# A graph layer's edge tables: edges sorted upwards, and the first blocks' tables, gathers, statistics and one-hots made beside the table stage

## Chip, cores and metric

One core of a Trainium2 chip. The metric is the device time of one execution in microseconds (us); lower is better.

## What is computed

The input is `x` (50000 nodes x 128), 25000 edges with a node `src` each and an attribute row `edge_attr` (25000 x 128), and the weights of a small network.

```
h   = relu(layernorm(x))
agg = segment_sum(edge_attr, src, 50000)          # edge rows added up per node
z   = silu(concat(h, agg) @ W1 + b1) @ W2 + b2    # 256 -> 256 -> 128
out = x + h + layernorm(z) * gamma + beta
```

`dst` is not used in the result. `src` is uniformly random over the nodes and not sorted.

## The kernel before

**Tiles and blocks.** Nodes are worked on in 49 blocks of 1024 (`BLOCK`), a block is 8 tiles, a half is 4 tiles. A tile is 128 nodes, or 128 slots for edge rows. There are NT = 392 tiles.

**Table stage (to 88 us).** Which edge rows belong to which tile must first be found out. The 25000 edges lie as 125 rows of EC = 200 columns. VectorE sorts each row by node: a key holds the node and the column, `largest` (MAX8) takes eight keys, `strike` (MATCH_REPLACE8) removes them. The sorted columns come in 50 groups of 4 (`STREAMS`). Since a sorted row of random nodes runs evenly through all nodes, column n needs only a window of the tiles (`WINDOWS`, at most 160 of 392); the largest nodes come first, so the windows go downwards. One `group_step(g)` on VectorE (L1001) makes the tile one-hots of group g (`hot_tile`, L1018), does its share of the sort and, for group g - 3 (`LAG_SLOT`), copies the ranks (L978), compares them with slot numbers (`is_slot`, L987) and multiplies with the edges' words (`hot_slot`, L996). TensorE does three matmuls for a column: `before` (L667) counts the edges of a tile in the rows above, `others` (L660, 4 columns later) adds the rest, the third (L673, 16 columns later) adds the word to a table in PSUM. ScalarE reads one rank per column out of the counts (L521). A loop of 200 + 16 columns on TensorE and of 200 on ScalarE, with waits on semaphores, keep the three in step. VectorE may run ahead until it meets the copy of ranks of group g - 3.

**Hand-over (88 to 110 us).** When the last column is through, ScalarE copies the last counts (L527), VectorE adds them up (`total_of`, L1040) and both copy the tables to SBUF (L1045, L537); ScalarE adds up how many edges found no slot (`excess_of`) and prepares the second layer's weights and the halves of the first's (`w1h`, means, `w2c`, `b2c`: L541 to L548). TensorE puts the words in their rows (L687), and VectorE makes from them the edge number of each slot: `table_words` and `edge_fields` for the first three blocks (24 tiles), then the first four tiles' edge numbers (`first_edge`, L1108), on which GpSimd starts four gathers (`gather_first`, L462). VectorE goes on with the statistics of block 0 (`statistics`, L871), `powers` (reciprocal square roots in 11 linked small steps and some more, L902 to L929; each linked step waits for the one before), `spill_flags`, `slot_tables`, the one-hots of block 0 (`one_hots`, L1122), and the low half of W1 (`w1l`, L1171). If an edge found no slot (it doesn't happen with these inputs), GpSimd adds up all edges one by one in HBM instead (`add_up_spill`). TensorE runs 24, 4 and 4 dummy matmuls (`keep_busy`, L693) ahead of and between its first pieces.

**Block stage.** For each half of a block TensorE turns h (`turn_h`, L702) and sums the gathered rows by one-hots (`sum_edges`, L717) into `za`; ScalarE rounds `za` to `hi` (L564, L566), VectorE makes the rest `lo` (`split_low`, L1132); TensorE's first layer takes `hi` and `lo` (`pre`, L731 to L736), ScalarE applies silu (L573), TensorE's second layer gives `y` (L756), ScalarE sums its squares (L603), and VectorE scales, adds h, x and beta (L1144, L1161, L1139, L1114). GpSimd gathers each tile's edge rows with one indirect DMA (L454). SyncE loads and stores blocks.

**What sets the order.** Each engine's program is a list written out by hand. An engine does its own list in order; a wait holds up all that stands behind it. The order of VectorE's list around the change is: all of `group_step`, totals and words, tables, L1164 to L1176, then `step(b)` from L1178, which for block 0 makes the word tables of the other 46 blocks, for block 1 their edge numbers.

Of the kernel before, what the change touches and what calls it, by code (L numbers as in the profile page):

```python
# [38 lines left out]
COLUMN_BITS = 8  # L39

# [59 lines left out]
def gnn_layer(nc, x, src, edge_attr, W1, b1, W2, b2, gamma, beta, out):  # L100
# [36 lines left out]
    assert SORTS[-1].stop == EC and WINDOWS[0].stop == NT  # L137
# [3 lines left out]
    with ExitStack() as ctx:  # L141
# [61 lines left out]
        first_part = sb("first_part", [P, HALF], F32)  # L203
        first_edge = sb("first_edge", [P, HALF], U32)
# [56 lines left out]
        dve_step, sort_step = sem("dve_step"), sem("sort_step")  # L261
        unpacked, fields_made, words_ready = sem("unpacked"), sem("fields_made"), sem("words_ready")
        w1h_ready, w1l_ready, means_ready, w2c_ready = sem("w1h_ready"), sem("w1l_ready"), sem("means_ready"), sem("w2c_ready")
# [109 lines left out]
        def _(pool):  # L373
            nc.gpsimd.memset(srci[:], OUTSIDE).then_inc(src_filled, 1)
            small_iota = dict(allow_small_or_imprecise_dtypes=True)
            nc.gpsimd.iota(column_no[:], [[1, EC]], base=1, channel_multiplier=0)
# [11 lines left out]
            for tiles_here in (WINDOWS[0], slice(0, WINDOWS[0].start)):  # L388
# [16 lines left out]
            def add_up_spill():  # L405

                pool.wait_ge(late_const, 1)
                rows_zeroed = P * TILES
# [37 lines left out]
            def gather(b, c, source, limit, pacer=None, signal=None):  # L446

                if b.is_number(FIRST_BLOCKS) and c == 0:
                    pool.wait_ge(slots_ready, 2)
# [9 lines left out]
            def gather_first(limit):  # L459

                for t in range(HALF):
                    nc.gpsimd.indirect_dma_start(  # L462
                        G[0][:, t, :], None, edge_attr,
                        bass.IndirectOffsetOnAxis(ap=first_edge[:, bass.ds(t, 1)], axis=0),
                        bounds_check=limit, oob_is_err=False).then_inc(first_gathered[t], 16)

            def gather_rest(source, limit):

                pool.wait_ge(slots_ready, 1)
                gather(Block(0), 1, source, limit)  # L470
                for c in range(2):
                    gather(Block(1), c, source, limit)

                def step(b):
                    if b.plus(2).exists(NB):
# [20 lines left out]
            with pool.If(flag != 0):  # L496
                spill_limit = pool.to_reg(NB * BLOCK - 1)
                add_up_spill()
                for t in range(HALF):
                    pool.wait_ge(first_gathered[t], 16)  # L500
                pool.wait_ge(slots_ready, 1)
                gather(Block(0), 0, spill, spill_limit, signal=gathered_anew)
                pool.wait_ge(gathered_anew, 16 * HALF)
# [5 lines left out]
        def _(act):  # L509
# [15 lines left out]
            run_columns(rank_of, 0)  # L525
# [8 lines left out]

            excess_of(0)
            act.wait_ge(slot_free, EC + UNROLL)
            nc.scalar.copy(words[:, 1, :], table[1][:, 0:NT]).then_inc(words_copied[1], 1)  # L537
            excess_of(1)

            act.wait_ge(weights_loaded, 16 * 6)  # L540
            nc.scalar.copy(w1h[:], w1f[:]).then_inc(w1h_ready, 1)  # L541
            for m in range(2):
                nc.scalar.activation(junk_w[:, m, :], w2f[:, m, :], ACT.Copy, scale=-1.0 / D, accum_out=w2mean[:, m:m + 1])
            nc.scalar.activation(junk_w[:, 2, :], b2f[:], ACT.Copy, scale=-1.0 / D, accum_out=b2mean[:]).then_inc(means_ready, 1)
            act.wait_ge(means_ready, 1)
            for m in range(2):
                nc.scalar.activation(w2c[:, m, :], w2f[:, m, :], ACT.Identity, bias=w2mean[:, m:m + 1])
            nc.scalar.activation(b2c[:], b2f[:], ACT.Identity, bias=b2mean[:]).then_inc(w2c_ready, 1)  # L548
# [39 lines left out]
            def bias(b, c):  # L588

                if b.is_number(0) and c == 0:  # L590
                    act.wait_ge(w2c_ready, 1)
# [713 lines left out]
```

## Time and profile before

| | us |
|---|---|
| median of three runs | 709.94 |
| lowest and highest | 709.68, 710.02 |
| the profiled execution | 710.16 |
| span of the profile in it | 708.6 |
| TensorE busy | 679.5 (96%) |
| VectorE busy | 688.1 (97%) |
| ScalarE busy | 608.5 (86%) |
| GpSimd busy | 479.6 (68%) |
| mean granted TensorE clock | 0.97 |

The profile covers one execution. The span runs from the first to the last instruction; the execution's own time is 1.56 us longer. PE is TensorE, PEld its weight loads, DVE is VectorE, ACT ScalarE, POOL GpSimd, SP SyncE. A busy time is the time in which records of an engine's instructions lie; records of neighbouring instructions may overlap by some 0.1 us. The granted clock is 1.00 for 2.4 GHz and 0.50 for 1.2 GHz. Times in a timeline row are its start and its length in us.

### The profile page before, as it was taken

The page shows a single profiled execution, that of the slowest core. Times are in us where ns is not written, and L with a number is a line of the kernel's source. Part 1 is how long each engine was busy: PE and PEld are TensorE (multiplying, and loading weights), DVE is VectorE, ACT ScalarE, POOL GpSimd, SP SyncE. Part 2 cuts the span into 40 slices and gives each one's busy share as a digit, 9 for nine tenths or more (in the row PEclk, how much of TensorE's full clock was granted, in tenths as well). Part 3 has the DMA queues.
Part 4 walks back from the last instruction along what each step waited for, and adds up shares of the span by engine and source line. Part 5 has one row for each costly group of instructions (what it writes and reads, how often), then busy time and mean ns, then how long its engine had stood idle before and what let it go on. Part 6 is the DMA issues. An engine that isn't in the chain of part 4 may idle for free.

```text
span 708.6 us, 15614 instructions
## 1 busy us (share of the span) xinstructions
PE 679.5 (96%) x4566; PEld 597.0 (84%) x4566; DVE 688.1 (97%) x2361; ACT 608.5 (86%) x2090; POOL 479.6 (68%) x416
## 2 busy tenths in 40 slices
PE   5999988799999999999999999999999999999993
PEld 3888847698998989898989898999998989899983
DVE  8999879999999999999999999999999999999998
ACT  7999957598898989898989898989898989889883
POOL 5000057687777787777778787778787778777850
PEclk7799979899999999999999999999999999999997
DMA  6000001133333333332424242424232423331212
GB/s 221 1 1 2 1 16 53 52 123 101 118 108 112 111 106 122 95 130 83 140 84 141 83 141 83 140 83 141 84 138 85 132 92 123 104 106 53 81 42 84
DMA packets 28260, 65.90 MB, mean 93 GB/s; under 512 B 8469, under 2 KB 10023, under 8 KB 28174
## 3 DMA queue, kind: packets, MB, share of 16 engines
q1 hardware_dynamic: 15598, 51.90, 20.7%
q0 software_dynamic: 12576, 12.99, 7.6%
q8 instruction: 37, 0.61, 0.4%
q14 instruction: 49, 0.40, 0.2%
HBM read 52.05 MB, written 25.60 MB: 110 GB/s over the span
## 4 chain that ended last, share of the span: by engine, by line
DVE 67%; issue 20%; PE 11%; ACT 1%; DMA 0%; DVEq 0%; POOL 0%; POOLq 0%
DVE T L1144 14%; DVE lo L1132 10%; DVE stat L871 10%; DVE R L1114 8%; DVE R L1139 8%; PE y L673 3%; DVE R L1161 2%; PE za L660 2%; PE pre L667 2%; PE pre L660 2%; PE za L667 1%; DVE guess_off L924 1%; PE pre L693 1%; DVE mdd L907 1%; DVE var L910 1%
## 5 line engine op out<-in xcount | busy, mean ns | idle before, releaser
L454 POOL DMA_INDIRECT G<-in_edge_attr_dram,slot_edge x388 | 465.7, 1200 | 121.0 <-issue 90.2
L756 PEld LDWEIGHTS y<-w2c,S 128*128 128x128 f32 (+1 forms) x1556 | 188.2, 191 | 8.0
L756 PE MATMUL y<-w2c,S 128*128 128x128 f32 (+1 forms) x1556 | 189.2, 275 | 0.0
L556 ACT ACTIVATE H<-X,shift,rstd 128x128 f32<-128x128 f32 x392 | 161.9, 489 | 4.4 <-DVE shift L929 4.4
L731 PE MATMUL pre<-hi,w1h 128*128 128x512 f32 (+1 forms) x392 | 163.8, 418 | 0.0
L732 PE MATMUL pre<-hi,w1l 128*128 128x512 f32 (+1 forms) x392 | 154.6, 394 | 0.0
L573 ACT ACTIVATE S<-pre,b1c 128x512 f32<-128x512 f32 (+1 forms) x196 | 125.4, 700 | 4.5 <-PE pre L736 4.5
L736 PE MATMUL pre<-lo,w1h 128*128 128x512 f32 (+1 forms) x392 | 123.1, 395 | 0.1
L1132 DVE TENSOR_TENSOR lo<-za,hi 128x1024 fp32r<-128x1024 f32 (+1 forms) x98 | 119.1, 1216 | 2.4 <-ACT hi L566 2.4
L871 DVE BATCH_NORM_STATS2 stat<-X 128x6 f32<-128x128 f32 x392 | 106.8, 281 | 0.1
L717 PE MATMUL za<-HOT,G 128*128 128x128 f32 (+1 forms) x784 | 104.7, 277 | 0.9 <-DMA G<-in_edge_attr_dram,slot_edge 0.9
L1144 DVE SCALAR_TENSOR_TENSOR T<-y,rstd,gammas 128x128 f32<-128x128 f32 x384 | 103.5, 342 | 0.0
L595 ACT COPY y<-b2c 128x512 f32<-128x512 f32 x97 | 59.1, 609 | 49.8 <-DVE T L1144 49.8
L603 ACT ACTIVATE junk_sq<-y 128x128 bf16<-128x128 f32 x388 | 99.7, 268 | 1.5 <-PE y L756 1.5
L717 PEld LDWEIGHTS za<-HOT,G 128*128 128x128 f32 x784 | 96.2, 193 | 1.7 <-DMA G<-in_edge_attr_dram,slot_edge 1.5
L736 PEld LDWEIGHTS pre<-lo,w1h 128*128 128x128 f32 x392 | 73.7, 188 | 18.7 <-DVE lo L1132 1.0
L731 PEld LDWEIGHTS pre<-hi,w1h 128*128 128x128 f32 x392 | 74.4, 190 | 13.5 <-ACT hi L566 0.3
L732 PEld LDWEIGHTS pre<-hi,w1l 128*128 128x128 f32 x392 | 74.3, 190 | 13.3
L603 ACT ACTIVATION_READ_ACCUMULATOR junk_sq<-y 128x1 f32 x388 | 78.8, 203 | 0.0
L566 ACT CAST hi<-za 128x512 fp32r<-128x512 f32 (+1 forms) x98 | 57.5, 587 | 16.2 <-PE za L717 16.2
L702 PE MATMUL za<-ident,H 128*128 128x128 f32 (+1 forms) x392 | 60.4, 277 | 6.7 <-DVE lo L1132 6.7
L564 ACT CAST hi<-za 128x512 fp32r<-128x512 f32 (+1 forms) x98 | 58.9, 602 | 6.2 <-PE za L702 6.2
(160 smaller groups left out, 953.2 us busy)
## 6 DMA issues: line engine op xcount, KB each, us to landing
X<-in_x_dram SPq DMA_DIRECT2D x48, 512.0 KB, 3.6
out_dram<-R SPq DMA_DIRECT2D x48, 512.0 KB
G<-in_edge_attr_dram,slot_edge POOLq DMA_INDIRECT x388, 2.6
X<-in_x_dram SPq DMA_DIRECT2D x1, 424.0 KB
out_dram<-R SPq DMA_DIRECT2D x2, 192.0 KB
w1f<-in_L_gnn_W_dram SPq DMA_DIRECT2D x1, 256.0 KB, 2.7
w2f<-in_L_gnn_W_dram SPq DMA_DIRECT2D x1, 128.0 KB, 2.7
srci<-in_src_dram SPq DMA_DIRECT2D x1, 87.5 KB
```

Source lines behind the costliest of these rows:

```text
L454: nc.gpsimd.indirect_dma_start(G[b.j][:, t, :], None, source, bass.IndirectOffsetOnAxis(ap=slot_edge[:, bass.ds(b.number(TILES, t), 1)], a ...
L556: done = nc.scalar.activation(H0[b.j][:, t, :], X[b.xj][:, t, :], ACT.Relu, bias=shift[b.j][:, t:t + 1], scale=rstd[b.ring(POWERS_LAG)][:, ...
L573: nc.scalar.activation(S[c][:, m, w], pre[m][:, w], ACT.Silu, bias=b1c[:, m:m + 1]).then_inc(silu_done, 1)
L603: done = nc.scalar.activation(junk_sq[:, p, c * HALF + t, :], y[2 * p + c][:, t * D:(t + 1) * D], ACT.Square, scale=float(D) ** -0.5, accu ...
L717: done = nc.tensor.matmul(za[:, 1, t * r:(t + 1) * r], G[b.j][:, c * HALF + t, :], HOT[b.j][:, c * HALF + t, 0:r], start=True, stop=True)
L731: nc.tensor.matmul(pre[m][:, w], w1h[:, k, cols], hi[c][:, k, w], start=(k == 0), stop=False)
L732: nc.tensor.matmul(pre[m][:, w], w1l[:, k, cols], hi[c][:, k, w], start=False, stop=False)
L736: done = nc.tensor.matmul(pre[m][:, w], w1h[:, k, cols], lo[c][:, k, w], start=False, stop=(k == 1))
L756: done = nc.tensor.matmul(places[t][0:r], S[c][:, m, t * r:(t + 1) * r], w2c[:, m, :], start=False, stop=True, skip_group_check=True)
L871: done = nc.vector.bn_stats(stats[b.ring(2)][:, t, :], X[b.xj][:, t, :])
L1132: nc.vector.tensor_tensor(out=lo[c][:, :, w], in0=za[:, :, w], in1=hi[c][:, :, w].bitcast(F32), op=ALU.subtract).then_inc(lo_done, 1)
L1144: done = nc.vector.scalar_tensor_tensor(out=T[c][:, t, :], in0=y[2 * b.ring(2) + c][:, t * D:(t + 1) * D], scalar=rstd[b.ring(POWERS_LAG)] ...
```

## The change

The edges are sorted upwards: the key is negated and brought above zero by a constant, and taken back when it is made an integer. The windows now start at tile 0 and end at tile 392. With that, the first three blocks' tiles (`FIRST` = 24) get no more edges after group READY - 1 (READY = 12, so EARLY_AT = 16, statistics from group 22, powers from group 30). At group 16 VectorE copies these 24 columns of the tables; TensorE places the words at column 64; VectorE makes the edge numbers in the steps of groups 17 to 21, the statistics of block 0 after groups 22 to 29, its powers around groups 30 to 40, its one-hots after that. GpSimd gathers all 24 tiles from `first_edge`. ScalarE prepares the weights beside columns 16 to 40. After the last column VectorE copies the other 368 columns and fixes the slots of blocks 1 and 2; 3 dummies stand where 24 stood, and the last 4 are gone.

```diff
-                first = max(0.0, 1.0 - middle - reach) * nodes
-                final = min(1.0, 1.0 - middle + reach) * (nodes - 1)
+                first = max(0.0, middle - reach) * nodes
+                final = min(1.0, middle + reach) * (nodes - 1)
+    FIRST = FIRST_BLOCKS * TILES
+    READY = max(g for g in range(GROUPS) if WINDOWS[g].start < FIRST) + 1
+    EARLY_AT = READY + LAG_SLOT + 1
+    EARLY_STEPS = 6
+    STATS_AT = EARLY_AT + EARLY_STEPS
+    POWERS_AT = STATS_AT + TILES
...
 # GpSimd
             def gather_first(limit):
-                for t in range(HALF):
+                for n in range(FIRST):
+                    b, t = Block(n // TILES), n % TILES
+                    done = first_gathered[t] if n < HALF else gathered[b.j][t // HALF]
                     nc.gpsimd.indirect_dma_start(
+                        G[b.j][:, t, :], None, edge_attr,
+                        bass.IndirectOffsetOnAxis(ap=first_edge[:, bass.ds(n, 1)], axis=0),
+                        bounds_check=limit, oob_is_err=False).then_inc(done, 16)
             def gather_rest(source, limit):
-                pool.wait_ge(slots_ready, 1)
-                gather(Block(0), 1, source, limit)
-                for c in range(2):
-                    gather(Block(1), c, source, limit)
...
 # ScalarE
-            run_columns(rank_of, 0)
+            def weights_beside(column):
+                for m in range(2):
+                    if column.is_number(16 + 4 * m):
+                        nc.scalar.activation(junk_w[:, m, :], w2f[:, m, :], ACT.Copy, scale=-1.0 / D, accum_out=w2mean[:, m:m + 1])
+                    if column.is_number(32 + 4 * m):
+                        nc.scalar.activation(w2c[:, m, :], w2f[:, m, :], ACT.Identity, bias=w2mean[:, m:m + 1])
+                if column.is_number(24):
...
+                if column.is_number(28):
+                    act.wait_ge(means_ready, 1)
...
+                if column.is_number(40):
+                    nc.scalar.copy(w1h[:], w1f[:]).then_inc(w1h_ready, 1)
...
+            normalise(Block(0), 0)
+            for s in range(PAIRS):
+                excess_of(s)
+            normalise(Block(0), 1)
             split_high(Block(0), 0)
...
 # TensorE
+            def place_words(at, copied):
+                for i in range(PAIRS):
+                    pe.wait_ge(words_copied[i], copied)
...
+                        done = nc.tensor.matmul(slot_word[w][:, at], to[rows, :], words[rows, s, at], **add)
...
+                if late.is_number(READY * STREAMS):
+                    pe.wait_ge(late_const, 1)
+                    place_words(slice(0, FIRST), 1)
...
             pe.wait_ge(totals_done, 2)
-            keep_busy(24)
+            keep_busy(3)
             turn_h(Block(0), 0)
             keep_busy(4)
+            pe.wait_ge(words_read, 2)
+            place_words(slice(FIRST, NT), 2)
             sum_edges(Block(0), 0)
-            keep_busy(4)
...
 # VectorE
             def as_integers(at, number):
-                nc.vector.tensor_copy(top_i[:, at], top[:, at]).then_inc(unpacked, 1)
+                nc.vector.tensor_scalar(out=top_i[:, at], in0=top[:, at], scalar1=-1.0, scalar2=float(KEY_TOP),
+                                        op0=ALU.mult, op1=ALU.add).then_inc(unpacked, 1)
...
                 # powers: behind each of its 11 linked steps
+                    if b.is_number(0):
+                        group_step(Item(POWERS_AT + place))
...
+            def copy_words(at, columns_done):
+                dve.wait_ge(slot_free, columns_done)
+                for s in range(PAIRS):
+                    nc.vector.tensor_copy(words[:, s, at], table[s][:, at]).then_inc(words_copied[s], 1)
...
                 # group_step: behind hot_tile
+                    if g.is_number(EARLY_AT):
+                        copy_words(first_tables, UNROLL + READY * STREAMS)
...
+            def early_tables(step):
...
+                if step == 1:
+                    dve.wait_ge(words_placed, 2)
+                    table_words(at)
...
+                elif step == 4:
+                    dve.wait_ge(early_step, 2)
...
+                    or_nowhere(first_edge[:], edge_f[:, at], at).then_inc(first_ready, 1)
...
+            for n in range(EARLY_AT):
+                group_step(Item(n))
+            for n in range(EARLY_STEPS):
+                group_step(Item(EARLY_AT + n))
+                early_tables(n)
             for t in range(TILES):
+                group_step(Item(STATS_AT + t))
                 statistics(Block(0), t)
             powers(Block(0))
-            spill_flags()
-            slot_tables(first_tables)
+            dve.wait_ge(early_step, 4)
+            dve.wait_ge(late_const, 1)
             one_hots(Block(0))
+            for n in range(POWERS_AT + SMALLS, GROUPS + LAG_SLOT):
+                group_step(Item(n))
+            dve.wait_ge(counts_copied, 1)
+            for s in range(PAIRS):
+                total_of(s)
+            copy_words(other_tables, EC + UNROLL)
             dve.wait_ge(w1h_ready, 1)
             nc.vector.tensor_tensor(out=w1l[:], in0=w1f[:], in1=w1h[:].bitcast(F32),
                                     op=ALU.subtract).then_inc(w1l_ready, 1)
+            for t in range(HALF):
+                statistics(Block(1), t)
+            spill_flags()
+            later = slice(TILES, FIRST)
+            link(nc.vector.tensor_scalar(out=slot_node[:, later], in0=slot_node[:, later], scalar1=kept[:],
+                                         scalar2=own_slot[:], op0=ALU.mult, op1=ALU.add))
+            for t in range(HALF, TILES):
+                statistics(Block(1), t)
             split_low(Block(0), 0)
-            for t in range(TILES):
-                statistics(Block(1), t)
             powers(Block(1))
```

Also changed, for the case of an edge without a slot: `add_up_spill` waits for the early gathers and sets tables and one-hots anew, and all three blocks are gathered again.

## Rows read from the trace of the kernel before

**Rows 1.** Windows, one block: us; busy PE, PEld, DVE, ACT, POOL; clock, DMA, GB/s.
```profile
307.73:319.70 11.97, 11.97 (x83) 10.77 (x82) 11.90 (x39) 10.62 (x35) 9.53 (x8) 1.00 0.34 109
```
**Rows 2.** Chain that ended last, hand-over: start us, us, what.
```profile
91.27 7.93 PE pre L693 x24
...
101.42 0.59 ACT hi L566
102.04 1.23 DVE lo L1132
...
108.85 1.23 DVE lo L1132
...
110.85 0.23 PE pre L731
```
**Rows 3.** Waits of VectorE in 8 to 89 us: total us, times, longest.
```profile
DVE rank L978 <- ACT junk_rank L521: 2.2, 8, 0.4
```
**Rows 4.** Timeline of the table stage: groups 16, 17, 41, 49; column 47; last `hot_slot`.
```profile
32.11 0.46 DVE L1018 TENSOR_TENSOR hot_tile<-iota_tile,tile_of 128x608 f16<-128x608 f16 x1
32.41 0.32 PE L673 MATMUL y<-hot_tile,hot_slot 128*128 128x152 f16 x1
33.38 0.49 DVE L1018 TENSOR_TENSOR hot_tile<-iota_tile,tile_of 128x640 f16<-128x640 f16 x1
...
72.83 0.43 DVE L1018 TENSOR_TENSOR hot_tile<-iota_tile,tile_of 128x544 f16<-128x544 f16 x1
...
84.10 0.25 DVE L1018 TENSOR_TENSOR hot_tile<-iota_tile,tile_of 128x192 f16<-128x192 f16 x1
...
88.05 0.42 DVE L996 TENSOR_TENSOR hot_slot<-is_slot,word 128x512 f16<-128x512 f16 x1
```
**Rows 5.** Timeline, VectorE in the hand-over: prices of the moved work.
```profile
94.11 0.17 DVE L903 SCALAR_TENSOR_TENSOR m<-stat 128x8 f32<-128x8 f32 x1
94.19 0.17 DVE L905 TENSOR_TENSOR mdif<-stat 128x8 f32<-128x8 f32 x1
...
103.18 1.63 DVE L871 BATCH_NORM_STATS2 stat<-X 128x6 f32<-128x128 f32 x8
...
105.48 1.22 DVE L1122 TENSOR_TENSOR HOT<-iota_node,slot_node 128x1024 f32<-128x1024 f32 x1
```
**Rows 6.** ScalarE: windows (columns as in rows 1), then timeline, first and last of its weight work.
```profile
14.00:20.00 6.00, 4.77 (x49) 3.92 (x48) 5.90 (x32) 5.50 (x32) 0.00 (x0) 0.50 0.51 200
20.00:25.00 5.00, 4.75 (x40) 4.45 (x41) 4.90 (x26) 4.59 (x26) 0.00 (x0) 0.51 0.01 3
...
90.84 0.60 ACT L541 CAST w1h<-w1f 128x512 fp32r<-128x512 f32 x1
...
92.97 0.39 ACT L548 ACTIVATE b2c<-b2f,b2mean 128x128 f32<-128x128 f32 x1
```
**Rows 7.** Windows of one us; the clock is the third number from the end.
```profile
86.00:87.00 1.00, 1.00 (x12) 0.49 (x10) 0.73 (x4) 1.00 (x10) 0.00 (x0) 0.67 0.00 0
...
96.00:97.00 1.00, 1.00 (x5) 0.36 (x4) 0.86 (x8) 0.26 (x1) 0.86 (x1) 0.71 0.16 32
...
130.00:131.00 1.00, 1.00 (x5) 0.76 (x4) 0.97 (x4) 1.00 (x5) 0.55 (x1) 0.64 0.00 0
```
**Rows 8.** Timeline, eight `za` matmuls at 2.4 GHz and at 1.2 GHz.
```profile
100.33 1.05 PE L717 MATMUL za<-HOT,G 128*128 128x128 f32 x8
...
126.81 1.92 PE L717 MATMUL za<-HOT,G 128*128 128x128 f32 x8
```
**Rows 9.** Waits of TensorE for gathered rows, 100 to 145 us.
```profile
PE za L717 <- DMA G<-in_edge_attr_dram,slot_edge: 0.5, 2, 0.3
```
**Rows 10.** Timeline, gathers on GpSimd beside VectorE in the block stage.
```profile
299.66 2.18 POOL L454 DMA_INDIRECT G<-in_edge_attr_dram,slot_edge  x1 [0.31 <-issue]
299.75 1.22 DVE L1114 TENSOR_TENSOR R<-X,betas 128x1024 f32<-128x1024 f32 x1
...
302.14 1.01 POOL L454 DMA_INDIRECT G<-in_edge_attr_dram,slot_edge  x1 [0.30 <-DVE lo L1132]
```

More of the change, by code:

```diff
@@ L407, in add_up_spill @@
                 pool.wait_ge(late_const, 1)
+                for j in range(RING):
+                    for c in range(2):
+                        if j or c:
+                            pool.wait_ge(gathered[j][c], 16 * HALF)
+                for t in range(HALF):
+                    pool.wait_ge(first_gathered[t], 16)
+                nc.gpsimd.tensor_copy(slot_edge[:, 0:FIRST], own_node[:, 0:FIRST]).then_inc(pool_step, 1)
+                nc.gpsimd.memset(G[RING - 1][:], 0.0).then_inc(pool_step, 1)
+                pool.wait_ge(hot_done, 1)
+                nc.gpsimd.tensor_copy(HOT[0][:], ident[:].unsqueeze(1).to_broadcast([P, TILES, P])).then_inc(pool_step, 1)
+                pool.wait_ge(pool_step, 8)
                 rows_zeroed = P * TILES
@@ L498, in _ @@
                 add_up_spill()
[L499 to L503, printed above, removed]
+                for n in range(FIRST_BLOCKS):
+                    for c in range(2):
+                        gather(Block(n), c, spill, spill_limit, signal=gathered_anew)
+                pool.wait_ge(gathered_anew, 16 * FIRST)
                 pool.sem_inc(way_known)
@@ L653, in _ @@
             pe.wait_ge(dve_const, 2)
+            def place_words(at, copied):
+                for i in range(PAIRS):
+                    pe.wait_ge(words_copied[i], copied)
+                for w in range(2):
+                    rows = slice(w * CAP, (w + 1) * CAP)
+                    for s in range(PAIRS):
+                        to = ident16 if w == s else swap16
+                        done = nc.tensor.matmul(slot_word[w][:, at], to[rows, :], words[rows, s, at], **add)
+                    done.then_inc(words_placed, 1)
             def column_step(column):
@@ L677, in _ @@
             run_columns(column_step, LAG_TABLE)
-            for i in range(PAIRS):
-                pe.wait_ge(words_copied[i], 1)
-            pe.wait_ge(late_const, 1)
-            for w in range(2):
-                rows = slice(w * CAP, (w + 1) * CAP)
-                for s in range(PAIRS):
-                    to = ident16 if w == s else swap16
-                    done = nc.tensor.matmul(slot_word[w][:, 0:NT], to[rows, :], words[rows, s, :], **add)
-                done.then_inc(words_placed, 1)
             def keep_busy(count):
@@ L1033, in _ @@
             tiles(SORTS[0], 0)
-            for n in range(GROUPS + LAG_SLOT):
-                group_step(Item(n))
-            dve.wait_ge(counts_copied, 1)
             def total_of(s):
```

94 lines of the change are left out of this document (49 added, 45 removed).

## The prediction

> **What bounds the kernel now.** I read the stretches first, then the chain of waits, then the engines' timeline around the two places where the chain changes hands.
>
> In the block stage (from about 140 us) a block takes 11.97 us; TensorE is busy for all of it and VectorE for 11.90 [rows 1]. The change touches nothing there, so it can only shift that stage. It must be judged by two spans ahead of it: the table stage, and the hand-over between it and the first blocks.
>
> The table stage ends on VectorE with the last `hot_slot`, at 88.05 + 0.42 = 88.47 us; call this E. The chain then runs through 24 dummy matmuls (7.93 us), block 0's aggregation and its rounding, and reaches `lo` of block 0's first half at 102.04 and of its second half at 108.85 [rows 2, 4]. From E to the first `lo` are 13.57 us, from the first to the second 6.81.
>
> In the table stage VectorE has hardly any slack: it waits for ranks 2.2 us in all [rows 3]. That idle time is the only cover for work put beside the columns. Group 17's `hot_tile` starts at 33.38, group 41's at 72.83, the last group's (49) at 84.10 [rows 4].
>
> **The change, part by part.** The order of the sort mirrors the windows: their widths add up to the same 6632 tiles over the 50 groups (worked out from the window formula). The key's sign and `as_integers` swap one instruction for one. I take 0, with nothing hidden. For that mirror image the first 24 tiles are complete after group 12, whence READY = 12, EARLY_AT = 16, statistics from group 22, powers from 30.
>
> *Added on VectorE in the table stage.* Statistics of block 0: eight in 1.63. One-hots of block 0: 1.14, from the record of 1.22 less the overlap of 0.08 with its neighbour. Small instructions follow each other by 0.08 [rows 5]; powers has 14, and since a group's step now stands between them their mutual waits go: 14 x 0.085 = 1.2. Early tables are 11 instructions, three of which read PSUM: 0.97. Sum 4.95. Two copies of 24 table columns at group 16: 0.25.
>
> *A new wait at group 16.* `copy_words` waits until the table matmul of column 47 is through. That one starts at 32.41 and takes 0.32; VectorE would be at that point 0.4 after `hot_tile` 16 at 32.11, so at 32.5 [rows 4]. It waits 0.3 even if nothing else moves. Everything of VectorE is queued behind it, `hot_tile` 17 first, for which TensorE then waits. TensorE in turn waits for the copies before four small matmuls; it has no lead to lose there that VectorE doesn't lose too, so I count no second time.
>
> *ScalarE's weight work beside columns 16 to 40.* It takes from 90.84 to 93.36 now, less a short wait, 2.3 us [rows 6]. In 14 to 25 us ScalarE is idle for 0.50 + 0.41 = 0.9 [rows 6], and TensorE needs a rank only four columns later. So between 0 (all hidden) and 1.4 (2.3 - 0.9) is passed on to TensorE and from it into VectorE's wait at group 16. I take 0.5, as the four columns between take up some half microsecond of the rest.
>
> *What goes.* With 4.95 more work VectorE runs behind ranks that are long there, and the 2.2 us of waits vanish. Between groups 17 and 41 it needs 1.64 us a group ((72.83 - 33.38) / 24, some waits included [rows 4]); with 1.0 more over five groups, 1.63 over eight and 1.2 over eleven it needs some 1.75 to 1.85. TensorE and ScalarE would have to need more than that for VectorE to meet a rank wait again, and then they would have held it up more than 2.2 us already.
>
> So E moves by 0.3 + 0.5 + 0.25 + 4.95 - 2.2 = **+3.8**, to 92.3.
>
> *From E to the first `lo`.* Now: totals 1.05 us after E, 24 dummies, `za` of the first half, `hi`. After the change, counted from E: totals done 1.05; three dummies; four transposes; four dummies; four matmuls that place the other words, 0.85; eight `za` matmuls. TensorE's granted clock fell to 1.2 GHz in 86 to 87 us, when the columns got narrow, and rose to 2.4 GHz in 96 to 97, when it had been busy without a gap since 91.2; after the idle time around 124 it rose in 130 to 131, busy since 125.9 [rows 7]. So most of this stretch runs at 1.2 GHz. A dummy costs 0.43 there (5.4 us of them at that pace and the remaining 2.5 at twice the pace make the 24), eight `za` 1.92 against 1.05 [rows 2, 8]. 7 x 0.43 = 3.0, transposes 0.9 (half of eight `za`), words 0.85, `za` some 1.3 with the clock rising inside them, latency 0.15, `hi` 0.6: 1.05 + 3.0 + 0.9 + 0.85 + 1.3 + 0.75 = 7.85, where 13.57 stood: **-5.7**. VectorE is there in time: two totals 0.95, two wide copies 0.9, `w1l` 0.6, eight statistics 1.63, spill flags and the fix of `slot_node` some 0.9, 5.0 after E. The gathers of block 0 are 24 x 1.31 = 31 us from group 20 on, at about 44, so done near 75; `way_known` then hangs on the spill flag alone, some 4.3 after E, under the dummies.
>
> *From the first to the second `lo`.* Eight statistics (1.63) have moved ahead into idle time. But the second half's `hi` isn't earlier by as much: by its own chain (`pre`, transposes, `za`, `hi`) it comes about 5.6 after the first `lo`, with the wait for gathered rows gone [rows 9]. 6.81 to 5.6: **-1.2**. Then TensorE sets `lo` of block 1's first half; there the lead shrinks by **0.5**. Behind that VectorE's own order (tables of the other blocks, statistics, powers) sets the pace as before, and the shift stays.
>
> Sum: 3.8 - 5.7 - 1.2 + 0.5 = **-2.6**. The profiled execution took 710.16 (span 708.6), 0.22 over the median of 709.94. 710.16 - 2.6 = 707.56; the median so 707.3.
>
> **A rule that speaks against the change.** Now 20 more gathers run on GpSimd beside VectorE's dense two-input work. In the trace a gather that starts just ahead of `R` (x plus beta) takes 2.18 instead of 1.01, and `R` its 1.22 as ever; VectorE isn't the one that waits [rows 10]. The Trainium skill, SBUF — State Buffer, "SBUF: two separate sides", says that the port pair shared by GpSimd and VectorE is an exclusive lock: whichever starts first has it for its whole instruction and the other blocks fully. By that rule VectorE would lose up to a gather's length each time; the rows agree for GpSimd as the loser and show no case of the other. My sum goes by the rows.
>
> **The rivals.**
> (a) *The table stage swallows more*: the added instructions fall into latencies between a group's own (a `hot_slot` starts 0.33 after its `is_slot`), and ScalarE passes nothing on. E moves by 1.5 to 2 only. For: VectorE isn't at work in each of those latencies. Against: they stay where they are, since the additions stand behind the group's step. 705.2.
> (b) *The clock or ScalarE's chain takes it back.* 21 of the first dummies and the last four are gone: if the clock rises only behind block 0's first `pre`, its 12 matmuls of 0.23 [rows 2] grow as the eight `za` do (1.92 / 1.05), by 2.3 us, or ScalarE's full 1.4 instead of 0.5 arrives. For: `za` at 126.81 shows what the low clock costs. Against: TensorE has hardly a gap in the stretch. 707.3 + 2.3 = 709.6 for the clock, 708.2 for ScalarE alone.
> (c) *Slower: VectorE blocked by the gathers in the table stage.* 24 gathers of 1.0 us each fall between groups 20 and 45. Each that blocks VectorE for more than 0.11 us on average (2.6 / 24) eats the gain, for more than 0.17 makes it slower by over 0.2%. At half of their length, 12 us: 719; at 0.2 us each: 712. For: the narrow ops there read two SBUF operands most of the time, so a gather will often be first. Against: rows 10, and VectorE's steady rows show the same durations with and without a gather.
> (d) *It doesn't do what it says*: the early gathers come so late that block 0 waits for them. They would need 50 us instead of 31, at more than 2.1 each; then `way_known` is late and the gain shrinks to nothing: 710.
>
> **How the numbers follow.** The forecast has 0.58, (a) 0.14, (b) 0.16, (c) 0.10, (d) 0.02. 0.2% (1.4 us) is about what a measurement of this kernel can tell from no change. Faster takes the forecast and (a) but for 0.02 of the forecast's edge, 0.70; same (b), (d) and that edge, 0.20; slower (c), 0.10. The forecast's own bounds are 706 to 708.9 (0 to 1.4 of ScalarE, 0.5 of pitches, 0.8 of the clock); the range reaches on to (a) and past (b): 704.7 to 710.7.
>
> **What the profile would show.** The last `hot_slot` ends near 92.3, and VectorE has no waits for ranks between groups 17 and 49 (waits there: the step on the table stage is wrong). At group 16 a wait of 0.3 to 1.7 of VectorE on TensorE. Gathers of 1.0 to 1.4 us between 44 and 80. The first `lo` near 100.2 and the second near 105.8; `lo` of block 1 near 111.6 instead of 114.24. The clock back at 2.4 GHz about 6.5 us after E. Blocks still 11.97 us. It is wrong if `hot_tile` or `hot_slot` records lengthen beside gathers, if `za` of block 0 waits for a DMA, or if the block stage's pace changes.

## The result and the profile after

The median after the change is **705.68 us** (four runs, 705.40 to 706.44) against 709.93 for the kernel before in the same comparison: a ratio of 0.9943, 95% interval 0.9931 to 0.9955. That is 4.25 us faster, where 2.6 was forecast. The profiled execution took 705.78, its span is 704.2 (before: 710.16 and 708.6), so the spans differ by 4.4.

The page of the kernel after, busy times:

```profile
PE 675.2 (96%) x4545; PEld 592.5 (84%) x4545; DVE 685.7 (97%) x2360; ACT 607.4 (86%) x2089; POOL 477.8 (68%) x416
```

The busy shares are those of before; nothing there tells where 4.4 us went. The stretches do. One block far inside the block stage, then the steps of one us behind the table stage (columns as in rows 1):

```profile
312.07:324.04 11.97, 11.97 (x82) 10.77 (x81) 11.90 (x39) 10.63 (x35) 9.53 (x9) 1.00 0.33 111
...
14.00:20.00 6.00, 5.20 (x49) 3.67 (x48) 5.89 (x32) 6.00 (x38) 0.00 (x0) 0.50 0.53 212
20.00:25.00 5.00, 4.49 (x37) 3.05 (x38) 4.90 (x26) 5.00 (x28) 0.00 (x0) 0.81 0.01 3
90.00:91.00 1.00, 1.00 (x12) 0.62 (x11) 0.77 (x3) 0.69 (x6) 0.00 (x0) 0.56 0.00 0
...
96.00:97.00 1.00, 1.00 (x5) 0.13 (x4) 0.72 (x4) 0.48 (x2) 0.00 (x0) 0.52 0.00 0
97.00:98.00 1.00, 1.00 (x10) 0.73 (x7) 0.00 (x0) 0.00 (x0) 0.00 (x0) 1.00 0.03 8
```

A block takes 11.97 as in [rows 1]. ScalarE, which had 0.9 us of idle time in 14 to 25 [rows 6], has none left: 6.00 of 6.00 and 5.00 of 5.00. The clock falls at the end of the table stage as it did [rows 7] and is back at 2.4 GHz (1.00) from 97 on, 5.4 us after the table stage's end.

VectorE's timeline of the kernel after: group 16 and the new wait, groups 17, 41 and 49, the last `hot_slot`, the spill flag, and the first, second, third and fifth `lo`. It answers to [rows 4] and [rows 2].

```profile
32.06 0.48 DVE L1058 TENSOR_TENSOR hot_tile<-iota_tile,tile_of 128x640 f16<-128x640 f16 x1
32.97 0.27 DVE L1039 CAST words<-y 128x24 f16<-128x24 f32 x2 [0.42 <-PE y L711]
...
34.04 0.48 DVE L1058 TENSOR_TENSOR hot_tile<-iota_tile,tile_of 128x640 f16<-128x640 f16 x1
...
77.68 0.43 DVE L1058 TENSOR_TENSOR hot_tile<-iota_tile,tile_of 128x544 f16<-128x544 f16 x1
...
87.78 0.25 DVE L1058 TENSOR_TENSOR hot_tile<-iota_tile,tile_of 128x192 f16<-128x192 f16 x1
91.15 0.42 DVE L1028 TENSOR_TENSOR hot_slot<-is_slot,word 128x512 f16<-128x512 f16 x1
95.21 0.15 DVE L1087 CAST spilled_i<-spilled 128x1 int32<-128x1 f32 x1
99.08 1.22 DVE L1155 TENSOR_TENSOR lo<-za,hi 128x1024 fp32r<-128x1024 f32 x1 [2.36 <-ACT hi L587]
104.49 1.22 DVE L1155 TENSOR_TENSOR lo<-za,hi 128x1024 fp32r<-128x1024 f32 x1 [0.58 <-ACT hi L587]
110.41 1.23 DVE L1155 TENSOR_TENSOR lo<-za,hi 128x1024 fp32r<-128x1024 f32 x1 [0.68 <-ACT hi L587]
...
129.01 1.22 DVE L1155 TENSOR_TENSOR lo<-za,hi 128x1024 fp32r<-128x1024 f32 x1
```

VectorE's timeline of the kernel before, the third and the fifth:

```profile
114.24 1.23 DVE L1132 TENSOR_TENSOR lo<-za,hi 128x1024 fp32r<-128x1024 f32 x1
...
133.28 1.22 DVE L1132 TENSOR_TENSOR lo<-za,hi 128x1024 fp32r<-128x1024 f32 x1
```

Call them `lo1`, `lo2`, `lo3` and `lo5`, and E the end of the last `hot_slot`, as in the prediction: 91.15 + 0.42 = 91.57. Then the account is

| stretch | before | after | change | forecast |
|---|---|---|---|---|
| start to E | 88.47 | 91.57 | +3.10 | +3.8 |
| E to lo1 | 13.57 | 7.51 | -6.06 | -5.7 |
| lo1 to lo2 | 6.81 | 5.41 | -1.40 | -1.2 |
| lo2 to lo3 | 5.39 | 5.92 | +0.53 | +0.5 |
| lo3 to lo5 | 19.04 | 18.60 | -0.44 | 0 |
| lo5 to the end of the span | 575.3 | 575.2 | -0.1 | 0 |

Two lines were missed: E moved by 0.7 less than forecast, and 0.44 us came in a stretch that I had declared untouched. The rest of the gap between 2.6 and 4.4 is spread over the hand-over.

The hand-over by TensorE's timeline of the kernel after:

```profile
92.84 1.46 PE L721 MATMUL pre<-zeros 128*128 128x512 f16 x3 [0.85 <-DVE total L1078]
94.10 1.06 PE L730 MATMUL za<-ident,H 128*128 128x128 f32 x4
94.95 1.91 PE L721 MATMUL pre<-zeros 128*128 128x512 f16 x4
96.80 0.39 PE L687 MATMUL y<-words,ident 64*128 64x368 f16 x1
...
97.27 1.16 PE L745 MATMUL za<-HOT,G 128*128 128x128 f32 x8
99.11 0.50 PE L759 MATMUL pre<-hi,w1h 128*128 128x512 f32 x1 [0.68 <-ACT hi L587]
```

From E: 1.27 to the first dummy, 1.26 for three, 0.85 transposes, 1.85 for four dummies, 0.47 words, then 1.16 for `za`, and 0.65 to `lo1`: 7.51.

VectorE's waits of the kernel after, 8 to 95 us and 95 to 152 us; they answer to [rows 3]:

```profile
DVE words L1039 <- PE y L711: 0.4, 1, 0.4
...
DVE lo L1155 <- ACT hi L587: 3.6, 3, 2.4
```

Before, the listed waits for ranks came to 2.2 us [rows 3]; after, one of 0.2 is left, and the wait at group 16 is new.

GpSimd's gathers of the three blocks, first and last of 24, none over 1.19 long:

```profile
42.27 1.16 POOL L482 DMA_INDIRECT G<-in_edge_attr_dram,first_edge  x1 [30.85 <-DVE first_edge L1114]
...
73.80 1.02 POOL L482 DMA_INDIRECT G<-in_edge_attr_dram,first_edge  x1 [0.31 <-issue]
```

### The profile page after: what moved, and what is told of

Same layout as the page of the kernel before. It is cut to its first block, busy times and chain, and to the rows that moved or that the text cites. A ratio compares the mean times of both kernels' runs of the same rounds, so it can differ in the third digit from the quotient of the medians.

```text
span 704.2 us, 15572 instructions
## 1 busy us (share of the span) xinstructions
PE 675.2 (96%) x4545; PEld 592.5 (84%) x4545; DVE 685.7 (97%) x2360; ACT 607.4 (86%) x2089; POOL 477.8 (68%) x416
## 4 chain that ended last, share of the span: by engine, by line
DVE 69%; issue 21%; PE 7%; ACT 2%; DVEq 0%; DMA 0%; POOL 0%; POOLq 0%
DVE T L1167 14%; DVE lo L1155 10%; DVE stat L901 10%; DVE R L1137 8%; DVE R L1162 8%; DVE R L1184 2%; ACT junk_rank L535 2%; PE y L711 1%; DVE guess_off L956 1%; DVE mdd L939 1%; DVE var L942 1%; PE pre L702 1%; DVE hot_slot L1028 1%; DVE keys L857 1%; PE za L695 1%
## 5 line engine op out<-in xcount | busy, mean ns | idle before, releaser
L472 POOL DMA_INDIRECT G<-in_edge_attr_dram,slot_edge x368 | 442.4, 1202 | 163.5 <-issue 84.4
```

Source lines behind the costliest of these rows:

```text
L472: nc.gpsimd.indirect_dma_start(G[b.j][:, t, :], None, source, bass.IndirectOffsetOnAxis(ap=slot_edge[:, bass.ds(b.number(TILES, t), 1)], a ...
```

## The experiments

Each run below starts from the kernel after (e6 from the kernel before, e8 to e11 from e3) and has its own comparison with the kernel before (709.88 to 709.95 in each). Medians, 95% intervals of the ratio, and where the profiled execution had E and the `lo`:

| run | us | ratio | E | lo1 | lo2 | lo3 |
|---|---|---|---|---|---|---|
| after | 705.68 | 0.9943 (0.9931 to 0.9955) | 91.57 | 99.08 | 104.49 | 110.41 |
| e1 weights behind | 707.96 | 0.9969 (0.9957 to 0.9982) | 91.33 | 101.34 | 106.74 | 112.65 |
| e2 24 dummies | 710.25 | 1.0003 (0.9993 to 1.0012) | 91.64 | 103.68 | 109.07 | 114.99 |
| e3 one-hots out | 705.14 | 0.9932 (0.9915 to 0.9948) | 90.48 | 98.20 | 103.59 | 109.50 |
| e4 gathers late | 709.00 | 0.9987 (0.9978 to 0.9997) | 91.35 | 100.45 | 107.23 | 113.15 |
| e5 no dummies | 707.60 | 0.9968 (0.9955 to 0.9980) | 91.61 | 99.11 | 106.41 | 112.32 |
| e6 upwards only | 709.84 | 1.0001 (0.9991 to 1.0011) | 88.50 | 101.74 | 108.54 | 113.95 |
| e7 statistics behind | 710.24 | 1.0007 (0.9998 to 1.0017) | 89.63 | 103.93 | 109.33 | 115.25 |
| e8 clock held high | 707.02 | 0.9968 (0.9958 to 0.9979) | 90.75 | 99.77 | 105.17 | 111.08 |
| e9 flag first | 705.37 | 0.9931 (0.9917 to 0.9944) | 90.52 | 98.81 | 104.21 | 110.12 |
| e10 flag first, clock held | 703.96 | 0.9916 (0.9903 to 0.9930) | 90.56 | 97.05 | 102.44 | 108.36 |
| e11 e10 with fewer dummies | 703.91 | 0.9919 (0.9906 to 0.9933) | 90.57 | 97.05 | 103.61 | 109.52 |

**e1: ScalarE's weights behind the columns again.** Is the gain paid for by ScalarE in the table stage?

```diff
             def column_step(column):
...
-                weights_beside(column)
...
+            act.wait_ge(weights_loaded, 16 * 6)
+            for n in (40, 16, 20, 24, 28, 32, 36):
+                weights_beside(Item(n))
```

> The changed kernel with ScalarE's weight work put back behind the last column (w1h first, then means, w2c, b2c), ahead of its normalise. Theory (the work costs the table stage nothing, and ahead of the transposes it would be in the way): E stays within 0.2 us of 91.57, and 2.3 us of weight work stand ahead of normalise and of the sums of missing slots, so the first lo comes 1.5 to 2 us later: 707.2 to 707.7. Rival (ScalarE's work in the table stage delays group 16 and is paid there): E comes 0.5 to 0.9 earlier, and the sum is 706.3 to 707.

E is 0.24 earlier and `hot_tile` of group 17 starts at 33.80 instead of 34.04, so this is what the weights cost in the table stage. Behind it they cost more. VectorE's timeline of e1:

```profile
96.67 0.21 DVE L1086 TENSOR_SCALAR spilled<-excess 128x1 f32<-128x1 f32 x1 [1.86 <-ACT junk_excess L569]
```

The weights push ScalarE's sums of excess edges back, VectorE stands 1.86 us for them, and the flag that lets `za` go comes at 96.92 instead of 95.21. The move of the weights is worth 2.28 us (707.96 less 705.68).

**e2: 24 dummies.** One number changed, `keep_busy(3)` to `keep_busy(24)`.

> The changed kernel with 24 dummies in place of 3. Theory (behind E TensorE's own list sets the first lo, the clock rises some 4 us after TensorE is busy without a gap): 21 more dummies, about 9 of them at 0.43 (the rest of the slow time, which the other work no longer needs) and 12 at 0.22 are 6.5 us, less 2.3 us that transposes, 4 dummies and words gain at the high clock: +4 to +4.5, 709.7 to 710.3, which is all the gain. Rival (the dummies are hidden under another wait, for the gathers' flag or for VectorE): under +1.5, below 707.2.

TensorE's timeline of e2:

```profile
92.90 7.31 PE L721 MATMUL pre<-zeros 128*128 128x512 f16 x24 [0.85 <-DVE total L1078]
```

`lo1` comes 4.60 us later and the whole gain is gone (710.25). With the statistics and powers made ahead, nothing is left for the 21 dummies to cover: they are simply in the way. Without the change of this one number the rest of the change brings nothing.

**e3: the one-hots of block 0 out of the table stage.** They go behind the copies of the words, where VectorE would otherwise wait for `hi`.

```diff
-            one_hots(Block(0))
             for n in range(POWERS_AT + SMALLS, GROUPS + LAG_SLOT):
                 group_step(Item(n))
...
             copy_words(other_tables, EC + UNROLL)
+            one_hots(Block(0))
```

> The changed kernel with the one-hots of block 0 (1.14 us of VectorE) taken out of the table stage and made behind the copies of the other words. Theory (VectorE sets the table stage and has 2.4 us to spare before the first lo): E comes 1.1 us earlier, the first lo too, 704.5 to 704.8. Rival (the one-hots were partly hidden in the table stage, or they are late for the first za): 705.4 to 706.

E is 1.09 earlier, close to the 1.14 of the instruction; `lo1` 0.88 earlier; the median 0.54 lower, though the intervals of the two ratios overlap, so that they alone don't show it. 1.14 us of work in the table stage costs the table stage 1.09: this addition behind a group's step found nothing to hide in.

**e4: the gathers start behind the totals.** 

```diff
+            pool.wait_ge(totals_done, 1)
+            gather_first(edge_limit, range(HALF))
...
+                gather_first(edge_limit, range(HALF, FIRST))
```

> The changed kernel with all 24 early gathers issued only when the totals are made: four, then the flag, then the other twenty, as the kernel before had them. Theory (the gathers cost VectorE nothing in the table stage, and are worth their wait behind it): E within 0.1 us of 91.57; the fourth gather ends 5.8 us after E and lands 2.5 us later, so the first lo comes 2 to 3 us later and the rows of the second half again some 1 us: 707.5 to 709. Rival (contention: the gathers beside the columns block VectorE): E comes 0.5 to 2 us earlier and part of the loss is won back: 706 to 707.5.

Two things come out of it. The first is rival (c): without 24 gathers in the table stage E is 0.22 earlier, 0.01 us for each gather. (Runs whose table stages are the same have E within 0.1 us of each other: 91.57, 91.64 and 91.61 in the kernel after, e2 and e5.) The second is what the early gathers bring: 3.3 us (709.00). TensorE's timeline of e4 shows the direct part, `za` in three pieces with 1.05 us of waits for rows:

```profile
97.06 0.71 PE L748 MATMUL za<-HOT,G 128*128 128x128 f32 x4
98.17 0.49 PE L748 MATMUL za<-HOT,G 128*128 128x128 f32 x2 [0.40 <-DMA G<-in_edge_attr_dram,first_edge]
99.31 0.49 PE L748 MATMUL za<-HOT,G 128*128 128x128 f32 x2 [0.65 <-DMA G<-in_edge_attr_dram,first_edge]
100.47 0.79 PE L762 MATMUL pre<-hi,w1h 128*128 128x512 f32 x1 [0.68 <-ACT hi L590]
```

The indirect part is in the last line: behind these waits TensorE's first `pre` takes 0.79 instead of 0.50, because the clock fell again (the windows of e4 have 1.00 in 99 to 100, 0.59 in 100 to 101, 0.50 in 101 to 103); lo1 to lo2 takes 6.78 instead of 5.41. And lo3 to lo5 takes 18.99 in e4 (lo5 at 132.14), against 18.60 after and 19.04 before. That is the stretch I had declared untouched.

**e5: no dummies at all.** Both `keep_busy(3)` and `keep_busy(4)` are taken out. Rival (b) by itself.

> The changed kernel without its three and four dummy matmuls behind the last column. Theory (they keep TensorE busy so that its clock is at 2.4 GHz for the first pre; without them transposes and words come earlier, but the gathers' flag holds the first za until about 4.3 us after E, with TensorE idle before it): the first lo 0.3 to 0.8 us earlier than at 99.08, but the clock rises only about 4 us later, the first 12 matmuls of pre run at 1.2 GHz, the second lo is 1 to 2 us later: 706.5 to 707.8. Rival (the dummies only delay): 704.2 to 705.

TensorE's timeline of e5, then its windows:

```profile
93.44 1.08 PE L730 MATMUL za<-ident,H 128*128 128x128 f32 x4 [1.41 <-ACT H L577]
...
96.38 2.08 PE L745 MATMUL za<-HOT,G 128*128 128x128 f32 x8 [1.13 <-POOLq L509]
99.13 0.80 PE L759 MATMUL pre<-hi,w1h 128*128 128x512 f32 x1 [0.68 <-ACT hi L587]
```

```profile
103.00:104.00 1.00, 1.00 (x4) 0.71 (x4) 0.80 (x5) 0.00 (x0) 0.00 (x0) 0.50 0.00 0
104.00:105.00 1.00, 1.00 (x9) 0.91 (x8) 0.00 (x0) 0.54 (x1) 0.00 (x0) 0.97 0.00 0
```

`lo1` isn't a hair earlier (99.11), though 3 us of dummies are gone. TensorE waits for ScalarE's H and then for the spill flag instead, which VectorE has at 95.39 and GpSimd passes on at 96.38. `za` so starts 0.89 earlier than with the dummies (97.27), but at 1.2 GHz it takes 2.08 instead of 1.16, and both end at the same time (98.46 and 98.43). TensorE then stays at 1.2 GHz up to 104, so `lo2` comes 1.9 later. The seven dummies delay `za` and give that back within it, and they buy 1.9 us behind it (707.60).

**e6: the kernel before, sorted upwards, and nothing else.** It has the diff's parts on `KEY_TOP`, the windows and `as_integers`.

> The kernel before with nothing but the order of the sort turned upwards (key, windows, back to an integer). Theory (the order is a mirror image and costs nothing by itself): 709.7 to 710.2, E within 0.2 us of 88.47. Rival (the narrower first windows help or the slower as_integers hurts): off by more than 0.5.

709.84, ratio 1.0001, E at 88.50 against 88.47: the order of the sort costs and brings nothing of its own. Its hand-over is that of the kernel before, yet from E to `lo1` it takes 13.24 instead of 13.57: the granted clock rose in 95 to 96 and not in 96 to 97. So 0.3 us of that stretch can differ from one execution to another.

**e7: statistics and powers of block 0 behind the words again.**

```diff
             for t in range(TILES):
                 group_step(Item(STATS_AT + t))
-                statistics(Block(0), t)
-            powers(Block(0))
...
             copy_words(other_tables, EC + UNROLL)
+            for t in range(TILES):
+                statistics(Block(0), t)
+            powers(Block(0))
```

> The changed kernel with statistics and powers of block 0 put back behind the copies of the words, the sums of missing slots ahead of normalise. Theory (2.8 us of VectorE in the table stage, 4.2 behind it because each small step waits for the one before, and there all on the way to the transposes): E 2.5 to 2.9 us earlier, near 88.9; the first lo 2.5 to 4 us later than at 99.08 counted in all, near 102: 707.5 to 709.5. Rival (TensorE's list sets the first lo, and the statistics fit beside it): below 705.7.

E is 1.94 earlier, `lo1` 4.85 later, and 710.24 is as slow as the kernel before (ten runs, 709.51 to 712.05). VectorE's timeline of e7 shows the price of the linked steps out of the table stage, 0.21 from one to the next, where [rows 5] had 0.08 for unlinked ones:

```profile
94.15 0.17 DVE L944 TENSOR_SCALAR guess<-var 128x16 int32<-128x16 int32 x1
94.36 0.17 DVE L947 SCALAR_TENSOR_TENSOR guess_sq<-guess 128x16 f32<-128x16 f32 x1
...
103.93 1.23 DVE L1153 TENSOR_TENSOR lo<-za,hi 128x1024 fp32r<-128x1024 f32 x1 [4.90 <-ACT hi L587]
```

Taken together, e1, e2, e4 and e7 show that each of four parts, taken back alone, costs 2.3 to 4.6 us: together 14.7, over three times what the change brings. They aren't independent gains. They are links in one path from E to `lo1` (VectorE's statistics, ScalarE's H and sums, GpSimd's rows, TensorE's list), and any one left in place takes back half of the gain or more.

**e8: the clock kept high by wide zero matmuls.** On top of e3. The prediction had most of the hand-over at 1.2 GHz; can it be had at 2.4?

```diff
+            def warm_step(column):
+                if column.n >= EC - WARM_COLUMNS:
+                    nc.tensor.matmul(slot_word[column.ring(2)][:, FIRST:NT], zeros16[:],
...
+                                     **add)
+                column_step(column)
+            run_columns(warm_step, LAG_TABLE)
```

The matmuls add zero, are 368 wide and stand in the steps from column 192 on; four more follow behind the loop.

> The kernel of e3_one_hots_out, with TensorE kept busy through the last columns: a matmul that adds zeros (368 columns) ahead of each step from column 192 on and four behind the last. Theory (between E and the first lo the low clock costs some 1.5 us and nothing else of TensorE is in the way but the gathers' flag): the granted clock stays at 1.00 past E, the first lo comes 6.2 to 6.6 us after E instead of 7.6: 703.7 to 704.4. Rival (the zeros delay the counts or the last tables, or the clock falls all the same): 705 or more.

The clock was 1.00 throughout and the time was worse, 707.02 (runs from 706.38 to 709.14). The last counts and the last tables finish later, and everything behind them: VectorE waits 0.61 us for the counts (e3: 0.17) and 0.77 for the tables (e3: not at all), and the flag comes at 96.83 instead of 95.25. TensorE's waits of e8:

```profile
PE za L757 <- POOLq L510: 1.8, 1, 1.8
```

That time TensorE stands for the flag, which VectorE makes behind those waits.

**e9: the flag first.** On top of e3 `spill_flags()` goes ahead of `w1l` and the statistics of block 1.

> The kernel of e3_one_hots_out with the flag for missing slots made right behind the one-hots, ahead of w1l and four statistics. Theory (two things end together ahead of the first za: TensorE's list with its dummies, and the flag, 1.0 us from VectorE over GpSimd to TensorE; e3 gained 0.9 of the 1.1 us because the flag held it 0.3): the flag comes 1.2 us earlier, TensorE's list alone is left, the first lo comes 0.3 us earlier than e3's 98.20: 704.4 to 704.9. Rival (the flag doesn't matter): as e3, 705.1.

Against e3 the flag is 1.34 us earlier (93.91 instead of 95.25), but `za` is no sooner: TensorE's own list is now the last to arrive, and in this profile it runs at 1.2 GHz to 97, where in e3's the clock rose in 95 to 96. TensorE's timeline of e9:

```profile
96.46 1.70 PE L745 MATMUL za<-HOT,G 128*128 128x128 f32 x8
```

The five runs lie in two groups, 704.24 and 704.54, and 705.37 to 705.77. The profile is of the second. That the clock rises sooner in the first is likely but no profile shows it. The ratio doesn't separate it from e3.

**e10: flag first and narrower zero matmuls.** On top of e9. The matmuls add zero as in e8, are 184 wide, one a step in steps 188 to 207, none behind the loop.

```diff
+            def warm_step(column):
+                if EC - 12 <= column.n < EC + 8:
+                    nc.tensor.matmul(slot_word[column.ring(2)][:, FIRST:FIRST + 184], zeros16[:],
...
+                                     **add)
+                column_step(column)
```

> e9_flag_first with 20 matmuls of 184 columns that add zeros, ahead of the steps of columns 188 to 207, where TensorE has room, and none behind. Theory (with the clock at 2.4 GHz and the flag early nothing else is in the way): E within 0.3 us of e3's 90.48, the first lo 6.3 to 6.8 us behind E instead of 7.6: 703.3 to 704.2. Rival (the clock falls all the same between column 207 and the dummies, or the zeros delay the counts as in e8): 704.6 or more.

TensorE's timeline of e10, and its windows:

```profile
95.23 1.16 PE L752 MATMUL za<-HOT,G 128*128 128x128 f32 x8 [0.72 <-POOLq L509]
```

```profile
90.00:91.00 1.00, 1.00 (x17) 0.96 (x15) 0.66 (x3) 0.98 (x2) 0.00 (x0) 1.00 0.00 0
```

703.96, and the five runs within 0.10 us: 1.7 faster than the kernel after (by three edits: e3's, e9's and these matmuls) and 5.9 faster than the kernel before. Against e9 the matmuls bring 1.4 by the medians. E is where e3 has it to 0.1 us (90.56 against 90.48), so the added matmuls cost the table stage next to nothing. VectorE goes into `lo1` at 97.05 without a wait, TensorE's wait for the flag is the 0.72 above. This version beats both kernels.

**e11: e10 with 2 and 1 dummies instead of 3 and 4.**

> e10_flag_warm with two and one dummies instead of three and four. Theory (at the high clock TensorE's list is 0.9 us shorter by this, but the flag and VectorE's own list to the first lo end about then, 6.2 to 6.4 us behind E): within 0.3 us of e10. Rival (the list still sets it, and the clock holds): 0.5 or more faster than e10; or the clock falls: 1 us or more slower.

`lo1` again at 97.05, but TensorE has 1.51 us of idle time ahead of `za` instead of 0.72. Windows of e11:

```profile
96.00:97.00 1.00, 0.40 (x4) 0.20 (x2) 0.97 (x5) 0.57 (x2) 0.00 (x0) 0.98 0.03 8
97.00:98.00 1.00, 0.93 (x2) 0.83 (x3) 0.95 (x1) 0.51 (x2) 0.00 (x0) 0.50 0.00 0
```

In the profiled run the clock fell at 97 and `lo2` came 1.17 later than in e10. Three runs of five took 703.83 to 703.91, two 704.93 and 705.16. As the profile is of one of the slower two (704.93), the four dummies that e10 has more are worth about 1 us in some executions and nothing in others; they are insurance, at no price that these times show (703.96 against 703.83 to 703.91).

## Why the prediction was right in sign and 1.7 us short

**The shape held.** What is lost in the table stage is won twice over in the hand-over, and the block stage only shifts. All four terms have the forecast sign. That the result lies in the range says little, as the range reached from 704.7 to 710.7 and held no change as well; the step by step account says more, and all its misses but one fell on the side of a larger gain.

**The table stage: +3.10 instead of +3.8.** Two terms were mis-sized, what ScalarE passes on and the waits that vanish. *Group 16:* `hot_tile` 17 starts 0.66 later, not 1.05 (0.3 of wait, 0.5 of ScalarE, 0.25 of copies). ScalarE's share was mis-sized: e1 measures 0.24, not 0.5, and the wait is 0.42 where 0.8 was added up. ScalarE took 0.9 of its 2.3 us in idle time; that most of the rest went into the four columns' lead is likely, but no run shows it. *Groups 17 to E:* the timelines give +3.02 from `hot_tile` 17 to 49 (53.74 against 50.72), less 0.58 from 49 to E, so +2.44, where the forecast had 4.95 - 2.2 = 2.75.

*The waits:* the 2.2 is what the view of waits lists, and it is short. VectorE's timeline of the kernel before, twice a `hot_slot` and the copy of ranks behind it:

```profile
77.37 0.42 DVE L996 TENSOR_TENSOR hot_slot<-is_slot,word 128x512 f16<-128x512 f16 x1
77.71 0.16 DVE L978 CAST rank<-rank 128x4 f16<-128x4 f32 x1
...
83.37 0.42 DVE L996 TENSOR_TENSOR hot_slot<-is_slot,word 128x512 f16<-128x512 f16 x1
84.02 0.17 DVE L978 CAST rank<-rank 128x4 f16<-128x4 f32 x1 [0.23 <-ACT junk_rank L521]
```

Without a wait the copy starts 0.34 after its `hot_slot`, while that one's record still runs. With a listed wait of 0.23 it starts 0.65 after it: the wait costs 0.31. At 82.78 it starts 0.44 after, and nothing is listed. Summed up so from group 17 to E, the waits cost 3.0 us before and 0.3 after; 2.8 went, not 2.2. The stretch from `hot_tile` 41 to 49, where nothing is added, shows the same: 11.27 before [rows 4], 10.10 after, 1.17 less, where 0.7 of waits are listed.

*The added work:* it is then 2.44 + 2.8 = 5.2 against 4.95. The gathers beside it, which the forecast had at nothing, are 0.2 of that by e4. So the instructions together were priced right to 0.1.

**E to lo1: -6.06 instead of -5.7.** The dummies took 3.11 against 3.0, the transposes 0.85 against 0.9, `za` 1.16 against 1.3. Off by more were the words, 0.47 against 0.85, and the start, 1.27 after E against 1.05. But the step "`way_known` then hangs on the spill flag alone, some 4.3 after E, under the dummies" hid how near the flag is. VectorE has the flag 3.79 after E, and GpSimd's answer takes another 1.0 (e5: 95.39 to 96.38), so `za` couldn't have gone ahead before 4.8 after E, against 5.70 in the list of TensorE. With two dummies less (an estimate, at 0.43 each) the two would end together. I had TensorE's list as the only path there; it was the longest by 0.9 us. Of the 0.36 as a whole, up to 0.3 can be the execution of the kernel before that was profiled (e6).

**lo1 to lo2, lo2 to lo3: -1.40 and +0.53** against -1.2 and +0.5: both as argued.

**lo3 to lo5: -0.44 instead of 0.** The step "behind that VectorE's own order sets the pace as before, and the shift stays" failed. Its order is the same and its pace isn't. Before, GpSimd still gathered blocks 1 and 2 there; after, those rows have long landed. The same instruction, with a gather running (kernel before) and with none (kernel after); VectorE and GpSimd of before first:

```profile
125.33 0.99 POOL L454 DMA_INDIRECT G<-in_edge_attr_dram,slot_edge  x1 [0.30 <-issue]
125.96 0.52 DVE L1071 TENSOR_SCALAR edge_row<-word_i 128x368 int32<-128x368 int32 x1
```

```profile
121.91 0.34 DVE L1104 TENSOR_SCALAR edge_row<-word_i 128x368 int32<-128x368 int32 x1
```

0.18 us for one instruction. The next largest is `var`, before (beside a gather from 115.38 to 116.38) and after:

```profile
115.99 0.37 DVE L910 TENSOR_SCALAR var<-meansq 128x8 f32<-128x8 f32 x1
```

```profile
112.11 0.17 DVE L942 TENSOR_SCALAR var<-meansq 128x8 f32<-128x8 f32 x1
```

Laid side by side, the two timelines part by 0.17 at `edge_row`, by 0.14 at `var`, and by 0.04 to 0.07 at three more instructions; that is the 0.44. e4 is the test: with the gathers put back beside this stretch it takes 18.99 again. All runs agree: with gathers there 19.04, 19.04 and 18.99 (before, e6, e4), without them 18.60 to 18.63 (after and the nine others). So the sentence of the prediction that the rows "show no case of the other", VectorE as the loser, was true of the rows I had read and not of the trace, and that VectorE's rows show the same durations with and without a gather doesn't hold here.

The Trainium skill, SBUF — State Buffer, "SBUF: two separate sides", has an exclusive lock of the shared port pair for the whole instruction of whichever starts first, for a VectorE instruction in a two-port mode, or for one with two SBUF inputs beside a GpSimd instruction that reads SBUF. No run here shows in which mode `edge_row` and `var`, with one tensor input each, ran. By that rule `edge_row` would have stood for the 0.36 us that were left of its gather and ended at 126.66; it ended at 126.48, and `var` ended at 116.36, no later than its gather. Nor do [rows 10] agree on who goes first: there the gather started 0.09 before `R`, and the gather was the one that took longer. VectorE does lose, but by 0.2 at most in this stretch and by 0.01 on average beside the 24 early gathers, so for its size the measurement decides.

**The rivals.** (a) gave 705.2, nearest to the result, for a reason that isn't so: E moved by 3.1 and not by 1.5 to 2, and e3 shows added work of 1.14 costing 1.09. Being near to the time was luck. (b) is real as a mechanism, as e5 shows with 1.9 us, but seven dummies are enough against it; ScalarE alone was 0.24. (c) is refuted in size by e4: 0.22 us in all, where over 2.6 were needed for it to be slower. (d) didn't happen: the gathers ran from 42.3 to 74.8, against 44 to 75 forecast.

What stays open: where ScalarE's weight work went that neither its idle time nor e1 accounts for, and why the clock rises sooner in some executions of e9 and e11 than in others.

## What to carry to other kernels

When work is moved out of a hand-over, go through every engine's path to the first instruction that all of them meet in: each part left in place (weights, statistics, gathers, filler) took back half or all of the gain here. Filler that keeps the clock up has to be sized again after each such move; here 24 dummies took back the whole gain, none lost 1.9 us, and 20 narrow matmuls put ahead of the place where the clock fell, with the flag made first and the one-hots moved behind, brought 1.7 us more. The flag that goes from VectorE through GpSimd to TensorE costs about 1 us though it is a single number (0.99 in e5, 0.98 in e10), so its maker belongs near the head of the list. And when waits are counted on as cover, take them from the starts in the timeline: here the list of waits gave 2.2 us and the starts 3.0.

## What was not expected of the hardware

- A flag made by VectorE (0.15 us) lets TensorE start 1.0 us later, by way of a branch on GpSimd (e5 95.39 to 96.38; e10 94.25 to 95.23).
- A gather on GpSimd lengthened one VectorE instruction from 0.34 to 0.52 us, while 24 gathers beside dense work cost 0.22 in all.
- Two versions, e9 and e11, run at two times each, about 1.2 us apart (704.2 to 704.5 and 705.4 to 705.8; 703.8 to 703.9 and 704.9 to 705.2). In the profile of e11 the clock falls, and `lo1` is at the same 97.05 as in e10; no profile of e11's faster executions was taken.
- The granted clock stayed at 1.00 through idle pieces of 0.5 us in 94 to 95 and 0.6 in 96 to 97 in e10, and fell to 0.50 at 97 in e11, where TensorE did nothing at all between 94 and 95.
- The table stage didn't feel TensorE's clock. In 8 to 20 us it was 1.00 in the profile of e3 and 0.50 to 0.52 in that of the kernel after, and `hot_tile` of group 17 started at 34.03 and 34.04.
